# Attention with the probabilities turned by a DMA round trip and block transposes on VectorE

## What is computed

```
x = x + conv_mixer(layernorm(x)); x = x + mixture_of_experts(layernorm(x))
x = x + attention(layernorm(x), ctx, seg);  x = x + ffn(layernorm(x))

# attention, 16 heads:
kv_c = kv @ W_kvc;  q_c = q @ W_dq
scores = (q_nope . k_nope + rope(q_c @ W_qr) . rope(kv_c @ W_kr)) / sqrt(192)
scores = where(seg - 8 <= key <= seg, scores, -1e30)
attn = softmax(scores)
out = einsum(attn, v) @ W_o
```

## Time and profile before

| | us |
|---|---|
| median of 3 runs (lowest, highest) | 3066.2 (3062.24, 3069.48) |
| the profiled execution's own time | 3065.81 |
| its span in the trace | 3064.0 |
| TensorE busy, share of the span | 3032.5, 99% |
| VectorE | 2248.4, 73% |
| ScalarE | 1379.9, 45% |
| GpSimd | 1224.1, 40% |
| chain that ended last: TensorE's share | 92% |

### The profile page before, as it was taken

One profiled execution on the slowest core, in us unless ns is written; L12 is line 12 of the kernel. 1 busy time (PEld: TensorE's weight loads), 2 busy tenths in 40 slices (PEclk: granted clock), 3 DMA queues, 4 the chain that ended last, 5 costly groups with the idle time before them and its releaser, 6 DMA issues.

```text
span 3064.0 us, 50062 instructions
## 1 busy us (share of the span) xinstructions
PE 3032.5 (99%) x18181; PEld 2636.4 (86%) x18181; DVE 2248.4 (73%) x5504; ACT 1379.9 (45%) x3399; POOL 1224.1 (40%) x1190
## 2 busy tenths in 40 slices
PE   9999999999999999999999999999999999999999
PEld 6777777899899799999999999999998788888887
DVE  7989999755677788888888888888887533333342
ACT  4655555433566455555555555555555211111111
POOL 9999999454333433333222333333311111111120
PEclk9999999999999999999999999999999999999999
DMA  4444442298899511111111111111102211111110
GB/s 153 131 144 138 129 130 86 86 307 299 220 265 284 189 49 49 49 49 43 49 42 49 49 49 36 49 38 47 49 29 81 88 56 55 55 49 43 46 42 14
DMA packets 179011, 292.41 MB, mean 95 GB/s; under 512 B 22616, under 2 KB 73952, under 8 KB 178768
## 3 DMA queue, kind: packets, MB, share of 16 engines
q1 hardware_dynamic: 145200, 193.24, 20.4%
q0 software_dynamic: 23344, 77.35, 7.9%
q10 hardware_dynamic: 10224, 18.62, 1.6%
HBM read 177.38 MB, written 111.76 MB: 94 GB/s over the span
## 4 chain that ended last, share of the span: by engine, by line
PE 92%; DVE 3%; DMA 2%; POOL 1%; ACT 1%; issue 1%; SPq 0%; POOLq 0%; DVEq 0%
PE f_Y L559 4%; PE t_U L1818 4%; PE f_Y L560 4%; PE f_Y L562 4%; PE t_U L1819 4%; PE t_U L1820 4%; PE g_O L2640 4%; PE g_PH L2628 4%; PE g_PH L2627 4%; PE g_PH L2626 4%; PE g_O L2642 4%; PE g_O L2641 4%; PE t_T L1794 3%; PE f_Y L554 2%; PE t_PO L1804 2%; PE t_PO L1805 2%
## 5 line engine op out<-in xcount | busy, mean ns | idle before, releaser
L1954 ACT ACTIVATE t_pr<-t_sm,t_nb 128x256 f32<-128x256 f32 x512 | 256.7, 502 | 418.5 <-DVE t_nb L2176 418.5
L2372 POOL TENSOR_TENSOR t_r<-t_r 128x256 f32<-128x256 f32 x128 | 95.8, 749 | 696.7 <-DVE t_r L2155 387.5
L2696 DVE CAST g_hh<-g_hf 128x512 fp32r<-128x512 f32 x128 | 67.8, 530 | 382.0 <-PE g_O L2642 380.2
L2667 ACT ACTIVATE g_hf<-g_PH,b1g 128x512 f32<-128x512 f32 x128 | 88.1, 688 | 528.3 <-PE g_PH L2628 457.0
L1360 POOL TENSOR_TENSOR c_kf<-c_vt,c_ct 128x512 f32<-128x512 f32 x256 | 284.5, 1129 | 5.9 <-ACT c_vt L775 3.2
L2186 DVE TENSOR_SCALAR t_pr<-t_pr,t_rw 128x256 f32<-128x256 f32 x512 | 256.7, 501 | 18.1
L559 PE MATMUL f_Y<-c_kh,c_th 128*128 128x512 f32 x540 | 250.8, 465 | 0.0
L562 PE MATMUL f_Y<-c_kl,c_th 128*128 128x512 f32 x540 | 213.7, 396 | 0.7 <-DVE c_kl L1072 0.7
L560 PE MATMUL f_Y<-c_kh,c_tl 128*128 128x512 f32 x540 | 213.4, 395 | 0.0
L2640 PE MATMUL g_O<-g_w,g_hh 128*128 128x512 f32 x512 | 200.1, 391 | 5.0 <-DVE g_hl L2698 5.0
L1818 PE MATMUL t_U<-t_voh,t_oth 128*128 128x512 f32 x512 | 202.0, 394 | 0.0
(11 more groups left out here) (375 smaller groups left out, 9974.9 us busy)
## 6 DMA issues: line engine op xcount, KB each, us to landing
xs<-c_zero SPq DMA_DIRECT2D x71, 256.0 KB, 4.6
f_xg<-xs SPq DMA_DIRECT2D x284, 64.0 KB
ys<-f_yt ACTq DMA_DIRECT2D x71, 256.0 KB, 5.1
f_xg<-xn SPq DMA_DIRECT2D x40, 256.0 KB, 4.9
c_xt<-x SPq DMA_DIRECT2D x32, 256.0 KB, 3.5
c_cr<-ctx SPq DMA_DIRECT2D x32, 256.0 KB, 4.0
c_ct<-ctxh SPq DMA_DIRECT2D x32, 256.0 KB, 4.9
c_t<-kt SPq DMA_DIRECT2D x32, 256.0 KB, 5.0
```

## The change

The probabilities are no longer turned on TensorE. ScalarE's exponentials stay in `sm`; VectorE takes only the reciprocals (`inverses`); ScalarE multiplies by them in a copy (`normalise`), which writes `pr` in an order (quarter i, key block k, query half t, 32 keys). SP stores `pr` to DRAM and loads it back with the quarters on the partitions (`probabilities`, two DMAs of 256 KB a head). Two steps after its scores VectorE turns the head in blocks of 32x32 (`pturn`) into `ptq` in SBUF; ScalarE copies the high part, VectorE subtracts the low part (`plow`), and `av` and `vo` come one step later than before. Keys and queries come out in another order: the copy of the keys into `kc` and four-part row DMAs (`residual`, `store`) account for it. The sequence's output is stored by SP in four parts; the mixed rows are kept by GpSimd. `krf` takes the place of `kc`, oth and otl have two buffers for three. GpSimd does gather and mix ahead of the rotations and spreads the mix over four steps. Six filling matmuls at N = 2 go. In the dense stage the first block's twelve matmuls are issued at TensorE's step 257, the splitting of the first weights moves one head, and the rows of the second group are sent and fetched two blocks earlier. The diff, cut to its core:

```diff
+    with ExitStack() as low:
+        m.ptq = sb(nc, low, "t_ptq", [128, 2, 2, 256])
     m.ptl = t("ptl", [128, 2, 2, 256], F32R)
-    m.oth = t("oth", [128, 3, 256], F32R)
-    m.otl = t("otl", [128, 3, 256], F32R)
+    m.oth = t("oth", [128, 2, 256], F32R)
+    m.otl = t("otl", [128, 2, 256], F32R)
     m.sm = t("sm", [128, 4, 256])
-    m.pr = t("pr", [128, 2, 2, 256])
+    m.pr = t("pr", [128, 2, 4, 2, 2, 32])
+    m.pq = t("pq", [128, 2, 512])
...
     def residual(b):
         if b:
-            w.wait_ge(*Q["to"]["out", b - 1])
+            w.wait_ge(*Q["to"]["out", b - 1, 3])
         else:
             w.wait_ge(*P["f", NH - 2])
             w.wait_ge(*A["wdqh"])
         if 0 < b < B - 1:
             w.wait_ge(*P["qcp", b + 1])
...
-        sp.dma_start(m.xo[:, :, :], halves_of(d["x2"][b])).then_inc(*Q["txo"]("xo", b))
+        w.wait_ge(*Q[kept(b)]["x2", b])
+        for c in range(4):
+            sp.dma_start(m.xo[32 * c:32 * c + 32, :, :], turned_rows_of(d["x2"][b], c)).then_inc(*Q["txo"]("xo", b, c))
+
+    def store(b):
+        w.wait_ge(*V["add", 2 * b + 1])
+        for c in range(4):
+            sp.dma_start(turned_rows_of(d["x3"][b], c), m.xo[32 * c:32 * c + 32, :, :]).then_inc(*Q["to"]("out", b, c))
+
+    def probabilities(N):
+        w.wait_ge(*A["nm", 2 * N + 1])
+        w.wait_ge(*V["pt", N - 4])
+        sp.dma_start(d["fp"][N % 4].rearrange("(i p f) -> p i f", i=4, f=128),
+                     m.pr[:, N % 2, :, :, :, :].rearrange("p i k t f -> p i (k t f)")).then_inc(*Q[f"ps{N % 2}"]("ps", N))
+        w.wait_ge(*Q[f"ps{N % 2}"]["ps", N])
+        w.wait_ge(*V["pt", N - 2])
+        sp.dma_start(m.pq[:, N % 2, :], d["fp"][N % 4].rearrange("(p l) -> p l", p=128)).then_inc(*Q[f"pl{N % 2}"]("pl", N))
...
+        if N >= 6 and (N - 6) % NH == NH - 1:
+            store((N - 6) // NH)
+        if 5 <= N < TOTAL and (N - 5) % NH == (12 if N - 5 < NH else 8):
+            residual((N - 5) // NH)
         if N < TOTAL and b + 2 < B:
             if h == 10:
                 load(b + 2)
             if h == 14:
...
+        if N < TOTAL:
+            probabilities(N)
...
-    def pturn(N):
-        w.wait_ge(*V["nm", 2 * N + 1])
-        w.wait_ge(*V["vw", 4])
-        w.wait_ge(*V["ptl", N - 1])
-        for kb in range(2):
-            for t in range(2):
-                i = pe.transpose(m.T[:, 256 * kb + 128 * t:256 * kb + 128 * t + 128], m.pr[:, N % 2, t, 128 * kb:128 * kb + 128], ident)
-        i.then_inc(*P("pt", N))
-
...
+        if N >= 5:
+            vo(N - 5)
...
-        if 1 <= N <= TOTAL:
-            pturn(N - 1)
-        if 2 <= N <= TOTAL + 1:
-            av(N - 2)
+        if 3 <= N <= TOTAL + 2:
+            av(N - 3)
         if N + EARLY < NH:
             weights(N + EARLY)
-        if N == 2:
-            keep_busy(pe, m.PU[0], ident, 6)
+        if N == TOTAL + 1:
+            dense_first(pe, w, K, 0, 0)
...
+        w.wait_ge(*V["krl", b - 1])
+        copy(m.kc[:, :].rearrange("p (k i f) -> p i k f", k=2, i=4), M.rearrange("p (i k f) -> p i k f", i=4, k=2)).then_inc(*A("kc", b))
...
-            w.wait_ge(*P["pt", N - 2])
...
-            ac.activation(m.pr[:, N % 2, t, :], m.sm[:, k4, :], ACT.Exp, bias=m.nb[:, k4, 0:1], scale=-1.0,
+            ac.activation(m.sm[:, k4, :], m.sm[:, k4, :], ACT.Exp, bias=m.nb[:, k4, 0:1], scale=-1.0,
...
+    def normalise(N):
+        w.wait_ge(*Q[f"ps{N % 2}"]["ps", N - 2])
+        for t in range(2):
+            x, k4 = 2 * N + t, (2 * N + t) % 4
+            w.wait_ge(*V["rc", x])
+            ac.activation(m.pr[:, N % 2, :, :, t, :], m.sm[:, k4, :].rearrange("p (i k f) -> p i k f", i=4, k=2), ACT.Copy,
+                          scale=m.rw[:, k4, 1:2]).then_inc(*A("nm", x))
+
     def pturn(N):
-        w.wait_ge(*P["pt", N])
-        w.wait_ge(*P["av", N - 2])
-        copy(m.pth[:, N % 2, :, :], m.T[:, :].rearrange("p (k c) -> p k c", k=2)).then_inc(*A("pth", N))
+        w.wait_ge(*V["pt", N])
+        copy(m.pth[:, N % 2, :, :], m.ptq[:, N % 2, :, :]).then_inc(*A("pth", N))
 
     def av(N):
         w.wait_ge(*P["av", N])
-        w.wait_ge(*P["vo", N - 3, 1])
-        copy(m.oth[:, N % 3, :], m.PO[:, 256 * (N % 2):256 * (N % 2) + 256]).then_inc(*A("oth", N))
+        w.wait_ge(*P["vo", N - 2, 1])
+        copy(m.oth[:, N % 2, :], m.PO[:, 256 * (N % 2):256 * (N % 2) + 256]).then_inc(*A("oth", N))
...
-        if N < TOTAL and r == 2 and 4 * (q4 + 1) < TOTAL:
-            qturn(q4 + 1)
-        if 1 <= N <= TOTAL:
-            pturn(N - 1)
         if 2 <= N <= TOTAL + 1:
-            av(N - 2)
+            pturn(N - 2)
+        if N < TOTAL:
+            normalise(N)
+            if r == 2 and 4 * (q4 + 1) < TOTAL:
+                qturn(q4 + 1)
+        if 3 <= N <= TOTAL + 2:
+            av(N - 3)
...
-        if N in (TOTAL - 5, TOTAL - 3, TOTAL - 1):
-            k = (N - TOTAL + 5) // 2
+        if N in (TOTAL - 4, TOTAL - 2, TOTAL):
+            k = (N - TOTAL + 4) // 2
...
+        w.wait_ge(*P["kvp", b])
...
+            w.wait_ge(*A["nm", x - 4])
...
-    def normalise(N):
+    def inverses(N):
         for t in range(2):
             x, k4 = 2 * N + t, (2 * N + t) % 4
             w.wait_ge(*A["ex", x])
-            w.wait_ge(*V["nm", x - 4])
             ve.reciprocal(m.rw[:, k4, 1:2], m.rw[:, k4, 0:1]).then_inc(*V("rc", x))
-            w.wait_ge(*V["rc", x])
-            ve.tensor_scalar(m.pr[:, N % 2, t, :], m.pr[:, N % 2, t, :], m.rw[:, k4, 1:2], None, ALU.mult).then_inc(*V("nm", x))
 
     def pturn(N):
+        w.wait_ge(*Q[f"pl{N % 2}"]["pl", N])
+        w.wait_ge(*P["av", N - 2])
+        ve.transpose(m.ptq[:, N % 2, :, :].rearrange("p k q -> p (k q)").rearrange("p (k c t) -> p c k t", k=4, c=4),
+                     m.pq[:, N % 2, :].rearrange("p (c k f) -> p c k f", c=4, k=4)).then_inc(*V("pt", N))
+
+    def plow(N):
         w.wait_ge(*A["pth", N])
-        ve.tensor_tensor(m.ptl[:, N % 2, :, :], m.T[:, :].rearrange("p (k c) -> p k c", k=2), f32(m.pth[:, N % 2, :, :]),
-                         ALU.subtract).then_inc(*V("ptl", N))
+        ve.tensor_tensor(m.ptl[:, N % 2, :, :], m.ptq[:, N % 2, :, :], f32(m.pth[:, N % 2, :, :]), ALU.subtract).then_inc(*V("ptl", N))
 
     def av(N):
         w.wait_ge(*A["oth", N])
-        ve.tensor_tensor(m.otl[:, N % 3, :], m.PO[:, 256 * (N % 2):256 * (N % 2) + 256], f32(m.oth[:, N % 3, :]), ALU.subtract).then_inc(*V("otl", N))
+        ve.tensor_tensor(m.otl[:, N % 2, :], m.PO[:, 256 * (N % 2):256 * (N % 2) + 256], f32(m.oth[:, N % 2, :]), ALU.subtract).then_inc(*V("otl", N))
...
-        if N >= 4 and (N - 4) % NH == NH - 1:
-            add_rows((N - 4) // NH)
+        if N >= 5 and (N - 5) % NH == NH - 1:
+            add_rows((N - 5) // NH)
...
                 qcomp(b + 1)
+        if 2 <= N <= TOTAL + 1:
+            pturn(N - 2)
         if N < TOTAL:
-            normalise(N)
+            inverses(N)
+        if 2 <= N <= TOTAL + 1:
+            plow(N - 2)
+        if N < TOTAL:
             if r == 2 and 4 * (q4 + 1) < TOTAL:
                 qturn(q4 + 1)
-        if 1 <= N <= TOTAL:
-            pturn(N - 1)
-        if 2 <= N <= TOTAL + 1:
-            av(N - 2)
+        if 3 <= N <= TOTAL + 2:
+            av(N - 3)
...
+    def keep(b):
+        w.wait_ge(*G["mix", b, 0])
+        w.wait_ge(*G["mix", b, 1])
+        gp.dma_start(halves_of(d["x2"][b]), m.xt[:, :, :]).then_inc(*Q["tx3"]("x2", b))
...
         q4, r = divmod(N, 4)
+        if b + 2 < B:
+            if h == 10:
+                gather(b + 2, 0)
+            if h == 11:
+                mix(b + 2, 0, (0,))
+            if h == 12:
+                mix(b + 2, 0, (1,))
+                gather(b + 2, 1)
+            if h == 13:
+                mix(b + 2, 1, (0,))
+            if h == 14:
+                mix(b + 2, 1, (1,))
...
-        if N >= 4 and (N - 4) % NH == NH - 1:
-            store((N - 4) // NH)
...
-        if b + 2 < B:
-            if h == 10:
-                gather(b + 2, 0)
-            if h == 12:
-                mix(b + 2, 0)
-                gather(b + 2, 1)
-            if h == 14:
-                mix(b + 2, 1)
+        if b + 1 < B and b and h in (7, 8):
+            turned(b + 1, h - 7)
...
+        r = k + 2 if g == 0 else k
+        if g + 1 < GROUPS and 6 <= r < 10:
+            dense_rows_out(sp, w, K, 4 * (g + 1) + r - 6)
+        if g + 1 < GROUPS and 7 <= r < 11:
+            dense_rows_in(sp, w, K, 4 * (g + 1) + r - 7)
...
-        if n < DSTEPS:
-            first(g, k)
+        if 0 < n < DSTEPS:
+            dense_first(pe, w, K, g, k)
```

104 lines of the change are left out of this document (48 added, 56 removed).

## The result

The changed kernel takes **3238.5 us** (3235.6 to 3240.8) against 3066.8 for the kernel before on the same chip: ratio 1.056, interval 1.054 to 1.058. The forecast was 3145 us. The sign was right and the range (to 3240) just holds the time, but the slowdown is 172 us and the forecast had 79.

What follows compares the result with a forecast made beforehand. The prediction took TensorE to bound the attention stage at 5.11 us a head. Its terms: 3065.8 + 82 (loop) + 3 (end) - 5 (dense-stage rows) = 3146, forecast 3145 us, range 3040 to 3240.

Steps and rivals of the forecast that it cites:

- TensorE as the bound before, its need after: Attention stage: TensorE sets 5.11 us a head before; without the probabilities' transposes (0.44) it needs 4.67.
- The loop: Each attention step: VectorE and ScalarE wait on one another in a circle, 5.43 us a head against 5.11, +82 us.
- the transpose: VectorE's block transpose of 512 columns in each head's step: 0.71 us, upper end 1.08.
- the pair of scaled copies: ScalarE's two normalising copies of 256 columns in each head's step: 0.42 us each, range 0.33 to 0.42.
- TensorE's busy share: Sign in the attention stage: falls to 4.67/5.43, about 86%, with idle time ahead of the scores.
- Cover 3.3 us; nothing is charged.: Probabilities' DMA write and read-back: done at 8.2 us, wanted at 11.5, so no cost.
- the trip: Probabilities' DMA write to DRAM and read back, each head: 2.4 and 2.9 us, 5.3 together, charged 0.
- rival C: Attention stage: probabilities come late behind big loads, four heads of 16 by 2 us, 128 us, 3273 us; chance 0.04.
- Residual and store ... under the same cover, 0.: Once a sequence on SP's queue: four issues each for residual and store, hidden behind other time, cost 0.
- plow, "nothing": VectorE's low-part subtraction each head: reading two SBUF tiles instead of PSUM takes 0.684 beside 0.69 us, no cost.
- +3: End of the attention stage: one head deeper, partly filled by twelve dense-stage matmuls; +3 us, between 0 and +8.
- -5: Dense stage: second group's rows sent two blocks earlier, removing waits; -5 us, between 0 and -6.

Runs made afterwards that it cites:

- the reordered kernels: Changed kernel, all parts kept, with engine order and lag within the step rearranged: 3032.9 us; the same with once-a-sequence loads set apart on SP's queue: 3015.6 us.

## Why the prediction was right or wrong

**TensorE as the bound before, its need after.** Right in the main. A kernel that is TensorE's again comes to 4.74 us a head for the 4.67 of the forecast. But with only part of the transposes gone, in the kernel before, 63 us came for 84, so other limits stood close by.

**The loop.** Right: 5.46 us a head where it stands alone, for 5.43; taking the normalising copies out of oth's way gave 123 us for 120. Its terms held too: the transpose measured 0.705 for 0.71, and the pair of scaled copies 0.80 to the next start for 0.84 (0.90 to its own end). The page's row for the latter:

```profile
L1980 ACT ACTIVATE t_pr<-t_sm,t_rw 128x256 f32<-128x256 f32 x512 | 228.9, 494 | 0.0
```

TensorE's busy share is 752/860 = 87% for the 86% forecast. This part is +0.35 x 256, some 90 us for 82.

**The step that failed: "Cover 3.3 us; nothing is charged."** Leaving the trip out of the changed kernel gives 56 us. I had taken the trip's median in a quiet stretch (2.4 and 2.9) and its cover in a mean step. The write took 6.7 us behind 1 MB of loads, and the odd steps are 3.5 us long, not 5.4. This was rival C, whose mechanism I named with its four late heads in sixteen and gave 0.04. In size it was wrong (128 us for 56); and it was no rival but a term: it comes on top of the loop, in a few steps of each sequence, whatever the rest does.

**"Residual and store ... under the same cover, 0."** Wrong in one place. ScalarE's copy into the rows tile waits for the store (12.5 us in 14 times). Without the trip in that queue step 6 is 1.0 us shorter. It is part of the 56.

**TensorE's clock** stood nowhere in the sum. The loop leaves TensorE idle, and behind one idle stretch of 2.67 us in a sequence it ran at its lower level, just ahead of work that others wait for; filling the stretch gave 20 us. In the trace shown the clock fell in nine of 14 such places, which accounts for 12 us, and in two other traces in 13. Before, the chain was "matmuls without a gap" and the granted clock was 1.00; the forecast put gaps into it and kept the clock.

**plow, "nothing".** Right, as far as the runs show. Median 0.693 for the 0.684 read; its mean is 0.771, since it is sometimes held up, to 1.8 us at most. But with GpSimd's mixing cut short, no step fell by it: VectorE only waited longer for oth.

**The end, "+3" and "-5".** The -5 came: behind 2545 us TensorE has no idle time, where it had 4.53. The +3 was far too low: the stretch behind the last scores is 11.8 us longer, so the term was about +17. TensorE's matmuls with the idle time ahead of them show where:

```profile
2515.25 0.77 PE L2664 MATMUL g_PH<-g_xh,g_w 128*128 128x512 f32 x1 [4.08 <-POOL g_w L2509]
...
2534.52 0.77 PE L2664 MATMUL g_PH<-g_xh,g_w 128*128 128x512 f32 x1 [6.92 <-ACT g_hf L2710]
2535.08 0.63 PE L2665 MATMUL g_PH<-g_xh,g_w 128*128 128x512 f32 x1
2535.51 0.63 PE L2666 MATMUL g_PH<-g_xl,g_w 128*128 128x512 f32 x1
```

11.0 us idle, some 3 more in front of av of heads 253 and 254, and behind the two gaps nine and twelve matmuls 0.43 us apart for 0.23, which is 1.8 and 2.4 us. My +3 counted the deeper pipeline and let the dense stage's matmuls fill it. I had not asked when their own weights are there, and they too are split one head later. The run with those matmuls moved has a tail 3.1 us shorter, with a new wait in front of the last av, so the order of that stretch is one part of it; the rest is read from the trace alone, and how the 17 us divide stays open.

**The sum, mended:** 3065.8 + 90 (loop) + 56 (trip) + 20 (clock) + 12 (tail) = 3244. Some of the tail is in the trip's 56 (without the trip the stretch behind the last scores is 3179.8 - 2450.5 = 729.3 us for 734.8), which leaves 3238, the time measured. That it fits to the microsecond is luck: trip and clock together gave 73 us and not 76, and the loop's 90 is itself read from the run without them.

**The rule weighed beforehand.** The Trainium skill ("VectorE: DVE Perf Modes", Rules for kernel authors) advises TensorE for a 128x128 transpose into PSUM, and so spoke against the change. Here the changed kernel is slower, but not for the reason of price: the reordered kernels, with the same block transpose and trip, are 32 and 51 us faster than the kernel before. By the 390 ns apiece of its section The three transpose paths, a row for bf16, TensorE would be rid of an estimated 1.56 us a head. No row here shows that: the fp32 transposes of the kernel before last 272 ns each and follow one another at 0.11 us, and the spacing at which TensorE is full fell by 5.11 - 4.74 = 0.37.

## What to carry to other kernels

When work moves to engines that have room, write the order of one step out for the engines that hand to one another and look for the loop: here engines at 75% and 61% busy set the pace, and nothing but order, one more head of lag and loads set apart brought the changed kernel from 3238 to 3016 us. A DMA put under a cover is to be costed in the step where the queue's largest transfers stand, against the shortest steps, not by medians; setting two large loads two steps apart gave back 17 us here. A forecast that leaves TensorE idle has to ask where the gaps fall and whose result is late when the clock is down; and each time an edit takes a wait away, ask which buffer or which consumer waits next (two of my own runs failed on that).
